# One attention-and-feed-forward layer on one core: the second turning of each round split between the weighings, and the output projection laid beside the first 96 lookup slots

## What is computed

```python
x = L0_attn_x                                   # (2, 1024, 1024)
x = _layernorm(x + attention(x, wq, wk, wv, wo))  # 32 heads of 32, rotary, causal softmax
Wg, Wu, Wd = (codebook[idx].reshape(idx.shape[0], -1) for idx in (idx_gate, idx_up, idx_down))
x = _layernorm(x + einsum('bsi,hi->bsh', silu(x @ Wg.T) * (x @ Wu.T), Wd))   # inner width 2752
```

## Time and profile before

| | us |
|---|---|
| median of three runs | 7037.45 (7036.92 to 7038.21) |
| the profiled execution, its own time | 7038.14 |
| span of the profiled execution, first to last instruction | 7036.0 |
| end of the attention, start of the output projection on PE | 1687.6 |
| first feed-forward product of the first step | 2404.3 |
| mean granted clock of PE, share of full speed | 0.996 |

### The profile page before, as it was taken

One profiled execution on the slowest core, in us unless ns is written; L12 is line 12 of the kernel. 1 busy time (PEld: TensorE's weight loads), 2 busy tenths in 40 slices (PEclk: granted clock), 3 DMA queues, 4 the chain that ended last, 5 costly groups with the idle time before them and its releaser, 6 DMA issues.

```text
span 7036.0 us, 109336 instructions
## 1 busy us (share of the span) xinstructions
PE 6852.8 (97%) x29072; PEld 4331.6 (62%) x29072; DVE 4982.9 (71%) x11788; ACT 3672.3 (52%) x6498; POOL 5063.2 (72%) x5316
## 2 busy tenths in 40 slices
PE   7999999999999999999999999999999999999998
PEld 3444666665466656666666666666666666666664
DVE  3320777775299877788877888778887788877864
ACT  0000777774177755555555555555555555555541
POOL 7777777777777777777777777777777777777760
PEclk9999999999999999999999999999999999999999
DMA  4232111112233323333332333333333233333321
GB/s 127 63 90 49 30 33 32 33 31 58 46 88 90 77 63 72 66 70 72 70 71 64 72 74 72 69 66 71 71 71 70 64 72 72 70 72 67 71 59 48
DMA packets 472442, 462.10 MB, mean 66 GB/s; under 512 B 231120, under 2 KB 347728, under 8 KB 467536
## 3 DMA queue, kind: packets, MB, share of 16 engines
q10 hardware_dynamic: 287072, 396.73, 20.0%
q0 software_dynamic: 169984, 22.10, 7.8%
q1 hardware_dynamic: 14832, 36.84, 1.4%
HBM read 398.07 MB, written 57.15 MB: 65 GB/s over the span
## 4 chain that ended last, share of the span: by engine, by line
PE 63%; DVE 2%; issue 1%; ACT 1%; DMA 0%; DVEq 0%; ACTq 0%
PE ps L414 33%; PE ps L442 17%; PE ps L460 9%; PE ps L425 4%; DVE onehot L964 1%; DVE picked L972 1%; PE ps L431 0%; ACT onehot L738 0%; ACT onehot L742 0%; PE ps L534 0%; DVE small L1015 0%; ACT arena L824 0%; DMA arena<-code_low 0%; DVEq L191 0%; DVE big L956 0%
## 5 line engine op out<-in xcount | busy, mean ns | idle before, releaser
L201 POOL DMA_INDIRECT raw<-in_codebook_dram,idx_sb x5312 | 5063.0, 953 | 1763.9 <-issue 1760.9
L414 PE MATMUL ps<-onehot,table 128*128 128x512 f32 x11776 | 3149.5, 416 | 55.4 <-DVE picked L972 28.7
L964 DVE TENSOR_SCALAR_CACHE_REDUCE onehot<-arena,small 128x512 fp32r<-128x512 f32 x3685 | 2514.1, 743 | 786.7 <-PE ps L414 759.2
L414 PEld LDWEIGHTS ps<-onehot,table 128*128 128x128 f32 x11776 | 2172.1, 188 | 944.3 <-issue 312.6
L738 ACT ACTIVATE onehot<-arena,small 128x512 fp32r<-128x512 f32 x2211 | 1435.4, 713 | 1078.7 <-PE ps L414 974.2
L742 ACT ACTIVATE onehot<-onehot,small 128x512 fp32r<-128x512 f32 x2211 | 1425.2, 708 | 0.0
L442 PE MATMUL ps<-big,arena 128*128 128x512 f32 (+1 forms) x2816 | 1281.2, 592 | 1.3 <-DVE big L956 1.3
L972 DVE SCALAR_TENSOR_TENSOR picked<-arena,small,ps 128x512 fp32r<-128x512 f16 x1472 | 1032.2, 743 | 52.7 <-PE ps L414 37.8
L442 PEld LDWEIGHTS ps<-big,arena 128*128 128x128 f32 (+1 forms) x2816 | 524.2, 187 | 514.0 <-issue 477.5
L877 DVE TENSOR_REDUCE small<-ps 128x1 f32<-128x384 f32 (+7 forms) x512 | 374.2, 752 | 434.7 <-PE ps L304 434.6
L460 PE MATMUL ps<-arena 128*128 128x512 f32 (+1 forms) x1408 | 646.0, 595 | 2.2 <-ACT arena L714 1.1
(11 more groups left out here) (70 smaller groups left out, 3117.4 us busy)
## 6 DMA issues: line engine op xcount, KB each, us to landing
arena<-code_low ACTq DMA_DIRECT2D x738, 256.0 KB
arena<-code_high ACTq DMA_DIRECT2D x738, 128.0 KB
raw<-in_codebook_dram,idx_sb POOLq DMA_INDIRECT x5312
gathered_units<-raw SPq DMA_DIRECT2D x40, 512.0 KB
arena<-gathered_units ACTq DMA_DIRECT2D x20, 1024.0 KB
queries_keys<-arena ACTq DMA_DIRECT2D x16, 1024.0 KB, 4.0
arena<-queries_keys ACTq DMA_DIRECT2D x32, 512.0 KB
big<-in_xT_dram ACTq DMA_DIRECT2D x4, 2048.0 KB, 17.4
```

Source lines behind the costliest of these rows:

```text
L201: pool.indirect_dma_start(raw[:, s, n, :], None, codebook, bass.IndirectOffsetOnAxis(ap=idx_sb[:, s, n:n + 1], axis=0),).then_inc(gathered ...
L414: last = mm(ps[:, bank + c, :], table[:, k, c, :], onehot[:, k, :], start=(k == 0), stop=(k == KLO - 1))
L964: dve.tensor_scalar(onehot[:, k, :], lo_sb[:, s % 2, :], kp_sb[:, k:k + 1], None, ALU.is_equal, ALU.add, accum_out=hits[:, k:k + 1]).then_ ...
```

## The change

Two parts, independent of each other.

1. `long_turned` gets a second buffer, chosen by the parity of the round. PE's long turning is split: groups 2 and 3 now stand between the short and the long weighing, groups 4 and 5 after the long one. ACT and DVE keep their order.
2. The stages "output projection" and "lookup slots" become one loop: 16 blocks of six slots. The 16 products of a block are dealt out over the slots as 4, 4, 3, 3, 2 and 0 (`PARTS`), each portion ahead of that slot's look-up. The projection always uses banks 0 and 1, the turning of its result banks 2 and 3, the look-up banks 4 and 5. So a look-up now waits for the picks of the slot before, not of the one before that. `norm_sums` of the block stands on DVE after the picks of slot 4, `norm` after those of slot 5, the square root on ACT in slot 5; the turning and its copy come in slots 1 and 2 of the next block. The loads of the codes are issued at the end of the attention.

```diff
+BESIDE = 3 * SLOTS // SB
+PARTS = (0, 4, 8, 11, 14, 16, 16)
...
-        long_turned = kb(32, 8).rearrange("p (o s t) -> p o s t", o=2, s=TB)
+        long_turned = kb(32, 16).rearrange("p (r o s t) -> p r o s t", r=2, o=2, s=TB)
...
-                if weighed:
-                    for o in range(2):
+                for o in range(2):
+
+                    if weighed:
                         weigh(i, u - 2, o, True)
-                if turned:
-                    turn(i, u - 1, 1)
+                    if turned:
+                        turn(i, u - 1, 1, (o,))
...
+            for k in range(SB):
+                for q in range(BESIDE):
+                    if PARTS[q] < PARTS[q + 1]:
+                        project(k, PARTS[q], PARTS[q + 1])
+                    unit, s = divmod(k * BESIDE + q, SLOTS)
+                    look_up(unit * SLOTS, s)
+                    if k == 0 and q == 0:
+                        pe.wait_ge(sel_ready, 1)
                     if s:
                         fold(unit * SLOTS, unit, s - 1)
                     elif unit:
                         fold(unit * SLOTS - SLOTS, unit - 1, SLOTS - 1)
+                    if k and q == 1:
+                        turn_x1(k - 1)
...
+            for k in range(SB):
+                for q in range(BESIDE):
+                    unit, s = divmod(k * BESIDE + q, SLOTS)
+                    look_up(unit * SLOTS, s)
+                    if q == BESIDE - 2:
+                        norm_sums(k)
+                    if q == BESIDE - 1:
+                        norm(k)
```

More of the change, by code:

```diff
@@ L305, in scores, with turn @@
                        start=False, stop=True).then_inc(scores_done, 1)
-            def turn(i, u, o):
+            def turn(i, u, o, heads=(0, 1)):
                 tb = round_of(u)[1][o]
-                for n in range(2):
+                for n in heads:
                     for c in range(1 + o):
@@ L375, in _, with project @@
                 weigh(PASSES - 1, ROUNDS - 1, o, False)
[L378 to L385 removed]
+            def project(k, n0, n1):
+                if n0 == 0:
+                    past(pe, sum_ready, k)
+                for n in range(n0, n1):
+                    h, g = divmod(n, NG)
+                    last = mm(ps[:, h, :], big1[:, g, k * P:(k + 1) * P], wo_sb[:, g, h * N:(h + 1) * N],
+                              start=(g == 0), stop=(g == NG - 1))
+                if n1 == 2 * NG:
+                    last.then_inc(wo_done, 1)
             def turn_x1(k):
                 pe.wait_ge(x1_ready, k + 1)
[L389 removed]
+                past(pe, x1T_ready, k)
+                if k == 0:
+                    pe.wait_ge(d_ready, 1)
                 for e in range(KT):
[L391 removed]
+                    last = nc.tensor.transpose(ps[:, 2 + e // 4, (e % 4) * P:(e % 4 + 1) * P],
                                                x1_blk[:, k % 2, e * P:(e + 1) * P], id_sb[:, :])
                 last.then_inc(x1T_done, 1)
[L395 to L402 removed]
             def look_up(first, s, bank=4, held=0):
@@ L486, in lookup_step @@
                         ffn_matmul(step, ni, n)
-            pe.wait_ge(d_in, 16)
-            for h in range(CS):
-                last = nc.tensor.transpose(ps[0:HALF, 2 + h // 4, (h % 4) * P:(h % 4 + 1) * P],
-                                           d_raw[:, h, :], id_sb[:, :])
-            last.then_inc(turn_done, 1)
-            pe.wait_ge(sel_ready, 1)
-            for unit in range(3):
-                for s in range(SLOTS):
-                    look_up(unit * SLOTS, s, 4 - 4 * (s % 2), 1)
+            pe.wait_ge(wo_in, 16)
+            pe.wait_ge(o_copied, 2 * ROUNDS * PASSES)
+            for k in range(SB):
[6 more added lines that the diff above has]
+                        pe.wait_ge(sel_ready, 1)
                     if s:
@@ L502, in _ @@
                         fold(unit * SLOTS - SLOTS, unit - 1, SLOTS - 1)
+                    if k and q == 1:
+                        turn_x1(k - 1)
+                if k == 0:
+                    pe.wait_ge(d_in, 16)
+                    for h in range(CS):
+                        last = nc.tensor.transpose(ps[0:HALF, 2 + h // 4, (h % 4) * P:(h % 4 + 1) * P],
+                                                   d_raw[:, h, :], id_sb[:, :])
+                    last.then_inc(turn_done, 1)
+            turn_x1(SB - 1)
+            pe.wait_ge(x1T_ready, SB)
             lookup_step(0, HALF, 3 * SLOTS, 3)
@@ L779, in _ @@
                 load_codes(0, s)
-            turned(1, HALF, 2)
-            act.wait_ge(sel_ready, 1)
+            act.dma_start(sel_raw, sel).then_inc(sel_in, 16)
+            act.wait_ge(unit_ready, 1)
+            act.dma_start(d_raw, units[0, :, 0:CS * HALF].rearrange("p (h i) -> p h i", h=CS)).then_inc(d_in, 16)
             near(0, 0)
-            for unit in range(3):
-                for s in range(SLOTS):
+            for k in range(SB):
+                for q in range(BESIDE):
+                    unit, s = divmod(k * BESIDE + q, SLOTS)
                     next_codes(unit, unit * SLOTS, s)
@@ L796, in _ @@
                         take(1, w_raw[:, 0, :])
+                    if k == 1 and q == 0:
+                        turned(1, HALF, 2)
+                    if k and q == 2:
+                        copy_x1(k - 1)
+                    if q == BESIDE - 1:
+                        deviation(k)
                     near(unit * SLOTS, s + 1)
+            copy_x1(SB - 1)
             lookup_step(0, HALF, 3)
@@ L924, in _, with norm_sums @@
                     copy_o(PASSES - 1, u, o)
-            for k in range(SB):
+            def norm_sums(k):
                 dve.wait_ge(wo_done, k + 1)
@@ L937, in _, with norm @@
                 dve.bn_aggr(meanvar, stats.rearrange("p n k -> p (n k)")).then_inc(var_ready, 1)
+            def norm(k):
+                past(dve, x1T_done, k - 1)
                 dve.wait_ge(std_ready, k + 1)
@@ L997, in _ @@
                 one_hot(0, 0, k)
-            for unit in range(3):
-                for s in range(SLOTS):
-                    look_up(unit * SLOTS, s, 4 - 4 * (s % 2))
+            for k in range(SB):
+                for q in range(BESIDE):
+                    unit, s = divmod(k * BESIDE + q, SLOTS)
+                    look_up(unit * SLOTS, s)
+                    if q == BESIDE - 2:
+                        norm_sums(k)
+                    if q == BESIDE - 1:
+                        norm(k)
             lookup_step(0, HALF, 3 * SLOTS)
```

45 lines of the change are left out of this document (10 added, 35 removed).

## The result

| | before | changed |
|---|---|---|
| median of the runs, us | 7037.5 (7036.9 to 7038.2) | 6947.2 (6945.0 to 6951.9) |
| ratio | | 0.9873, 95% interval 0.9855 to 0.989 |
| profiled execution, us | 7038.1 | 6948.9 |
| its span, us | 7036.0 | 6946.8 |
| first product of the projection, us | 1687.58 | 1639.24 |

The span lost 89.2 us. The last two lines of the table divide it. The attention ends 48.3 us earlier, and the stretch from the projection's first product to the first feed-forward product takes 675.6 us in place of 716.7, 41.1 less. The forecast had 48 and 43. All of the gain has arrived by 2315 us; what comes behind takes 4632 us in both.

The account below looks back on a forecast made before the run. PE was taken as the bound, so time is won where it idles or runs alone. Attention 48 plus projection and look-up 43 make 91 us, so 7038.1 - 91 = 6947 us (chance 0.52), range 6914 to 6994.

Parts of the forecast that it names:

- Part 1, what goes: Attention: PE's wait at group 4 for ACT's copy of group 2 goes, 0.625 us a round with run-out, together 80 us.
- Part 1, what comes: Attention: two more passages a round between turning and weighing cost 0.25 us a pair, leaving a gain of 48 us.
- Rival 1: Attention: passages between turning and weighing cost nothing, so part 1 gives 80 us; 6915 us, chance 0.12.
- rival 2: Attention: passages between turning and weighing drain in full, 0.44 us a pair; 6971 us, chance 0.10.
- Part 1, what is late next: Attention, round with the smallest wait: copy 2 is through 0.6 us before PE wants group 4, so no wait returns.
- rival 3: Attention: the copies' wait returns at another group because ACT's chain sets the round; part 1 gives 10, 6985 us, chance 0.07.
- Part 2, the block: Projection and look-up loop: six slots take 41.2 us, with 1.6 us of waiting in slot 5; 16 blocks 659 us.
- rival 4: Projection and look-up loop: DVE bounds the block, which takes 44 us; 6992 us, chance 0.09.
- rival 5: Projection and look-up loop: DVE's chain is hidden wholly, 39.4 us a block; 6918 us, chance 0.07.
- rival 6: Look-up slots: one-hots start only behind their slot's look-up, 8.6 us a slot; 7114 us, chance 0.03.
- Part 2, the seams: Around the 16 blocks: start 6.5, end 3.3 plus a slot of 4.1, taking out units 1.5; stretch 674 us, saving 43.
- The gathers: POOL's gathers keep their own pace: 91 us less leave 40 us of slack, and gains stop counting at about 130 us.

Follow-up runs that it names:

- e4_slot5_banks: Changed kernel with the look-up of slot 5 in banks 2 and 3, so it need not wait for slot 4's picks: 6930.4 us.
- e1_again: Kernel before with only the second long_turned buffer and the split turning, projection still ahead of the slots, run on another chip: 6991.3 us.
- e3_again: Changed kernel with one more pair of passages between turning and weighing in each round, run on another chip: 6998.1 us.
- e9_best: Changed kernel with turning in three stretches, the fourth row maximum ahead of the second normalisation, and products dealt 4, 3, 3, 2, 2, 2: 6903.3 us.
- e5_again: Changed kernel with turning in three stretches, one pair of passages fewer a round, run on another chip: 6934.5 us.
- e6_parts: Changed kernel with a block's 16 products dealt out as 4, 3, 3, 2, 2, 2 instead of 4, 4, 3, 3, 2, 0: 6927.4 us.

## Why the prediction was right, point by point

**The bound.** PE was the bound, and every gain here came from places where PE idled or ran alone. The reason given was weaker than it looked: the chain of the earlier trace rows begins at 2317 us, so its 63% said nothing of the two stages that were changed. What carried the argument there was the busy time of the earlier trace rows, and the 95% of e4_slot5_banks, whose chain is whole, confirms it.

**Part 1, what goes.** The 53.1 us ahead of the turning became 2.0. That the run-out of 0.21 us a round goes with it was argued from the rows; 48.1 us in e1_again can only be had with it, since the idle part alone less the passages (53 - 32) would be 21. With the 0.27 us of e3_again for the pair, the part that goes is 48 + 35 = 83 us; the forecast had 80.

**Part 1, what comes.** 0.25 us a pair of passages. The changed kernel's own rows give 0.22 to 0.28, e3_again 0.27 in the rounds without a returned wait, and with a pair removed e9_best gained 28 us in the attention (0.22 a round), e5_again 13.6 with 19 lost in another place. Rival 1 (no price, 6915) and rival 2 (a full drain, 6971) both fall. The Trainium skill (TensorEngine Tiling, Key Properties) says that a change of the tiling mode drains the engine. Every passage from 128x128 to 128x32 weights shown here does lose 0.09 to 0.14 us, so the trace agrees that there is a loss; what it doesn't show is the wait for the last product, which would be 0.22.

**Part 1, what is late next.** The walk left 0.6 us for copy 2, and no wait came back in the changed kernel: rival 3 falls there. It was a matter of half a microsecond, as e5_again shows.

**Part 2, the block.** Slot by slot, forecast and then measured, from the look-up's start: 7.57 and 7.30, 7.58 and 7.58, 6.71 and 6.68, 5.85 and 6.05, 5.75 and 5.84, and from slot 5 to slot 0 7.7 and 7.48. The sum was 41.2 and is 40.9. The forecast wait of 1.6 us in slot 5 is 1.33 by its row and 1.5 with the run-out ahead of it. The look-up of slot 0 is 0.27 late, behind the picks that follow VectorE's one-hots, where the prediction had 0.1 and named more than a tenth there as a sign of being wrong. It did no harm: VectorE's chain took 7.48 us from slot 5 to slot 0 and the forecast had 7.7, and the look-up is late only against PE, which would have needed 7.2 us and not 7.57. Rivals 4 (44 us a block), 5 (39.4) and 6 (slots of 8.6) fall. That the wait is made by the single pair of banks, e4_slot5_banks shows: with other banks and the same one-hot buffer it is gone, and 16 us with it. e6_parts shows that more work of PE ahead of the look-up covers it too, for 20 us.

**Part 2, the seams.** Here terms were mis-sized, and they cancel. Sixteen blocks of 40.9 are 654.9, so the seams are 675.6 - 654.9 = 20.7 us, where 15.4 stood.

At the end the forecast had 7.7 + 3.3 + 4.1 = 15.1 us from slot 95's look-up to the first feed-forward product; it took 2314.85 - 2297.44 = 17.4. Up to the next look-up all went well: 10.5 us in place of 11.0, with VectorE's one-hots and picks where the sum had them. But this look-up and its fold take 6.9 us where 4.1 stood, at a granted clock of 0.60 between 2308 and 2315. The prediction's own rows had the warning: in the kernel before, the same two take 2404.29 - 2398.39 = 5.9 us, and the sum took a slot from the middle of the steps instead.

In the middle 1.5 us stood for taking out finished units. Block 5 alone, in which ACT takes the first unit out, is 43.8 us from fold to fold, 2.9 more than its neighbours. ACT has its copy of the unit and that of x1 one behind the other, so it asks for the next codes late. From the chain that ended last:

```profile
1877.12 4.11 DMA arena<-code_low
...
1886.14 5.51 PE ps L412 x16
```

VectorE waits for these codes, its picks are late, and PE idles 2.01 us ahead of the look-up at 1886.14. That look-up takes 5.4 us to its fold and not 3.7, with a clock of 0.72. Three other blocks add 1.4 us, most of it where the first unit's entries are turned in the first block. Against all this stand blocks that were 0.3 us shorter than forecast, 16 of them, some 4 us. So the stretch came out at 675.6 for a forecast of 674 in part by luck, and the hit on 6947 to a fraction of a us is luck altogether: the runs of the changed kernel lie between 6945 and 6952.

**The gathers.** 40 us of slack were forecast at 91 us of gain; in the changed kernel there were 75, from the last gather's issue at 6796.68 to the product that reads it at 6872.13. The forecast took POOL's end as fixed, and it is not. The last gather was issued at 6826 us in the kernel before, at 6796 or 6797 in e1_again and the changed kernel, at 6846 in e3_again, at 6822 and 6823 in e4 and e5, and at 6811 or 6812 in e6 and e9. It does not follow the length of the kernel, and no run here says what it follows. So "gains stop at about 130 us" was no fixed line; e9_best has gained 134 and doesn't wait.

## What to carry to other kernels

Look how far back the chain of a page reaches before its shares are read as the bound of a stage. Price a change of the order of instructions at the passages that the trace already has: the start of the next kind of work less the count times the spacing inside the kind. Then look at what the moved piece used to cover, down to half a microsecond. Three times here (e3_again, e5_again, slot 5) a short wait on another engine appeared exactly where a covering piece had become shorter than that engine's chain. Where work is dealt out in portions beside a chain of fixed length, give each slot just enough to cover the chain rather than most to the first. And take the cost of a seam from rows at a seam, not from the middle of a loop.

## What was not expected of the hardware

**The clock fell after a short rest.** At the last seam PE idled 1.37, 3.91 and 1.10 us between 2296 and 2308, and the granted clock from 2305 to 2315 was 0.66, so part of that time at 1.2 GHz in place of 2.4. In block 5 it was 0.72 from 1886 to 1892, behind 2.01 us of idle time. Behind the 1.33 us that slot 5 waits it stayed at 1.00 (2172 to 2182). Before, with 2.31 us of idle time at the same place, it was 0.81 between 2396 and 2405. Stretches of the changed kernel around the seam:

```profile
2290.00:2305.00 15.00, 10.46 (x42) 7.28 (x40) 13.67 (x34) 10.62 (x18) 11.34 (x13) 1.00 0.30 56
2305.00:2315.00 10.00, 8.16 (x27) 6.22 (x28) 4.96 (x12) 1.06 (x2) 7.56 (x9) 0.66 0.23 43
```

The look-up that follows takes 6.36 us to its fold, not 3.7, so this seam costs its idle time and 2.7 us more.

**One chip was twice as slow.** On it PE waited on "issue" and had half the clock as long as POOL's gathers ran, and a gather took 1.05 or 1.06 us on average in place of 0.95. The kernel before took 13645 us there too, and no kernel did so on the other chips. No run here explains it.
